# A planned attention-and-FFN kernel: the low-bits branch moves into the first batch's list, and the step lists are reordered

## The reference

```python
qkv = x @ Wqkv + bqkv
att = softmax(where(causal, q @ k.T * D ** -0.5, -inf))
x = layernorm(x + (att @ v) @ Wout + bout)
h = silu(lin(x, w1)) * lin(x, w2)          # lin: (x @ w.T) * s
h = gelu(lin(h, h1)); h = gelu(lin(h, h2))  # 1024 -> 1024
x = layernorm(x + lin(h, w3))
```

## Time and profile before

| | us |
|---|---|
| median of three runs | 2191.09 |
| fastest and slowest run | 2189.73, 2191.16 |
| the profiled execution | 2188.74 |
| its span | 2187.0 |
| PE busy in it | 2129.8 (97%) |
| ACT, DVE, POOL busy | 1317.0, 1248.7, 489.7 |

### The profile page before, as it was taken

One profiled execution on the slowest core, in us unless ns is written; L12 is line 12 of the kernel. 1 busy time (PEld: TensorE's weight loads), 2 busy tenths in 40 slices (PEclk: granted clock), 3 DMA queues, 4 the chain that ended last, 5 costly groups with the idle time before them and its releaser, 6 DMA issues.

```text
span 2187.0 us, 52042 instructions
## 1 busy us (share of the span) xinstructions
PE 2129.8 (97%) x16294; PEld 1873.9 (86%) x16294; DVE 1248.7 (57%) x3928; ACT 1317.0 (60%) x2807; POOL 489.7 (22%) x899
## 2 busy tenths in 40 slices
PE   7679999999999999999999999999999999999998
...
DMA packets 95941, 167.71 MB, mean 77 GB/s; under 512 B 19204, under 2 KB 38404, under 8 KB 95672
## 3 DMA queue, kind: packets, MB, share of 16 engines
...
...
## 4 chain that ended last, share of the span: by engine, by line
PE 88%; issue 1%; ACT 1%; SPq 1%; DVE 1%; DMA 1%; POOL 0%; ACTq 0%; DVEq 0%; POOLq 0%
PE ring L1236 44%; PE ring L1221 11%; PE pM L1111 7%; PE pS L1099 6%; PE pO L1159 6%; PE ring L1249 5%; PE ring L1171 4%; PE ring L1201 2%; PE ring L1191 2%; ACT probs_a L766 1%; PE ring L1143 1%; SPq L606 0%; DMA Qs<-nm 0%; PE ring L1210 0%; DMA rec<-rec_d 0%
## 5 line engine op out<-in xcount | busy, mean ns | idle before, releaser
L916 DVE CUSTOM_DVE_ANT_0 pM<-pM,mask 128x512 f32<-128x512 f32 (+3 forms) x1024 | 497.8, 502 | 361.6 <-PE pM L1111 298.9
L1236 PE MATMUL ring<-Yhi,H 128*128 128x256 f32 x1984 | 501.8, 290 | 0.3 <-DVE c L932 0.3
L1236 PE MATMUL ring<-Xhi,H 128*128 128x256 f32 x1984 | 497.7, 289 | 0.0
L1236 PE MATMUL ring<-Ylo,H 128*128 128x256 f32 x1984 | 487.4, 282 | 0.0
L1236 PE MATMUL ring<-Xlo,H 128*128 128x256 f32 x1984 | 486.1, 282 | 0.0
L1236 PEld LDWEIGHTS ring<-Yhi,H 128*128 128x128 f32 x1984 | 377.1, 190 | 10.6 <-issue 6.5
L1236 PEld LDWEIGHTS ring<-Ylo,H 128*128 128x128 f32 x1984 | 378.0, 190 | 6.8 <-issue 3.3
L1236 PEld LDWEIGHTS ring<-Xlo,H 128*128 128x128 f32 x1984 | 379.3, 191 | 1.4
L1236 PEld LDWEIGHTS ring<-Xhi,H 128*128 128x128 f32 x1984 | 378.4, 191 | 1.5 <-issue 0.2
L1111 PE MATMUL pM<-Ks,Qs 128*128 128x512 f32 x992 | 301.1, 343 | 16.1 <-DVE mx L916 9.4
L860 ACT ACTIVATE Yhi<-ring,cols 128x256 fp32r<-128x256 f32 x248 | 117.1, 472 | 277.3 <-PE ring L1236 155.8
...
## 6 DMA issues: line engine op xcount, KB each, us to landing
...
```

Source lines behind the costliest of these rows:

```text
L916: nc.vector.tensor_tensor_reduce(pM[:, h % 2, 0:n], pM[:, h % 2, 0:n], mask[:, T - n:T], 1.0, NEG, ALU.add, ALU.max, mx[:, t, h:h + 1]).th ...
L1236: mm = nc.tensor.matmul(to, w, x_part, start=(k == 0 and m == 0), stop=(k == KB - 1 and m == 1))
```

## The change

`weight_flag` becomes the last entry of HEAD_ORDER. The branch then stands inside pass 0: PE runs HEAD up to and with `weight_flag`, reads the flag, and each of the two variants begins with the rest of HEAD (`among=slice(flagged, None)`) and goes on with pass 1 as a whole. `ends` is replaced by a test on the slice. The ring bank of `weight_flag` is given out with the others of HEAD and no longer set by hand.

All three lists have a new order. ORDER has the same 326 steps. HEAD has three steps that were not in it, `x1_turn:0:1`, `exp:1:1:3` and `weight_flag:0`, and no longer has `o_out:1:0`, `max:1:2:3:0` and `max:1:2:3:1`, which are now in FIRST. TAIL_ORDER is as it was.

The code, and of the lists the stretches around the branch, around ffn_out and gu, and of the end of attention (the diff is cut):

```diff
 ORDER = """
...
-h_act:-2:h2:1:5 qk:0:3 h2:-2:1:6:0 ln1:-1 h_rest:-2:h2:1:6 h2:-2:1:6:1 neg_max:0:1 stack:0:3 h_act:-2:h2:1:6
-h_act:-2:h2:1:7 h_rest:-2:h2:1:7 h2:-2:1:7:0 h2:-2:1:7:1 x1_turn:-1:0 max:0:2:3:0 ffn_out:-2:1:0 ffn_out:-2:1:1
-table:0:Exp:2 exp:0:1:0 exp:0:1:1 max:0:2:3:1 x1_turn:-1:1 exp:0:1:2 exp:0:1:3 max:0:2:3:2 exp:0:1:4 max:0:2:3:3
-exp:0:1:5 gu:-1:0:0 exp:0:1:6 gu:-1:0:1 exp:0:1:7 ffn_hi:-1:0:0 gu:-1:0:2 exp:0:1:8 ffn_hi:-1:0:1 max:0:2:2:0
...
-h1:-1:0:6:1 h_rest:-1:h1:0:4 h_rest:-1:h1:0:5 h_act:-1:h1:0:6 neg_max:0:2 h_rest:-1:h1:0:6 h_act:-1:h1:0:7
-h1:-1:0:7:0 max:0:3:3:0 h_rest:-1:h1:0:7 table:0:Exp:4 max:0:3:3:1 h1:-1:0:7:1 qk:1:0 max:0:3:3:2 h2:-1:0:0:0
-exp:0:2:0 exp:0:2:1 h2:-1:0:0:1 o_out:0:1 exp:0:2:2 max:0:3:3:3 exp:0:2:3 max:0:3:2:0 h2:-1:0:1:0 exp:0:2:4
...
-h2:-1:0:7:0 h_rest:-1:h2:0:5 h2:-1:0:7:1 neg_max:0:3 h_rest:-1:h2:0:6 h_rest:-1:h2:0:7 qk:1:1 ffn_out:-1:0:0
...
-exp:0:3:9 ffn_hi:-1:1:5 gu:-1:1:7 exp:0:3:10 ffn_hi:-1:1:6 ffn_hi:-1:1:7 v:1:0 pv:0:3:1 max:1:0:2:0 max:1:0:2:1
-o_out:0:3 table:0:Gelu:7 h1:-1:1:0:0 h_act:-1:h1:1:0 v:1:1 den:0 max:1:0:2:2 max:1:0:2:3 h1:-1:1:0:1 h1:-1:1:1:0
-max:1:0:1:0 stack:1:1 h1:-1:1:1:1 max:1:0:1:1 h_rest:-1:h1:1:0 h_act:-1:h1:1:1 h1:-1:1:2:0 h_act:-1:h1:1:2
...
-h1:-1:1:6:1 neg_max:1:0 h1:-1:1:7:0 h_act:-1:h1:1:6 h_act:-1:h1:1:7 h1:-1:1:7:1 h_rest:-1:h1:1:4
-h_rest:-1:h1:1:5 neg_split:1:0 den_turn:0 h_rest:-1:h1:1:6 ln2:-1:0 qk:1:2 h_rest:-1:h1:1:7
+max:0:1:3:0 max:0:1:3:1 y:-1:0:0 table:0:Exp:0 exp:0:0:0 y:-1:0:1 max:0:1:3:2 max:0:1:3:3 exp:0:0:1 y:-1:1:0
...
+h2:-2:1:4:1 h_rest:-2:h2:1:3 neg_split:0:1 ln1:-1 qk:0:3 h_act:-2:h2:1:5 h2:-2:1:5:0 h2:-2:1:5:1 h2:-2:1:6:0
+h_rest:-2:h2:1:4 neg_max:0:1 h_rest:-2:h2:1:5 h_act:-2:h2:1:6 o_out:0:0 max:0:2:3:0 h_act:-2:h2:1:7
+h_rest:-2:h2:1:6 h2:-2:1:6:1 h2:-2:1:7:0 h2:-2:1:7:1 max:0:2:3:1 h_rest:-2:h2:1:7 x1_turn:-1:0 table:0:Exp:2
+ffn_out:-2:1:0 x1_turn:-1:1 exp:0:1:0 exp:0:1:1 ffn_out:-2:1:1 exp:0:1:2 max:0:2:3:2 exp:0:1:3 gu:-1:0:0
+exp:0:1:4 max:0:2:3:3 exp:0:1:5 gu:-1:0:1 exp:0:1:6 ffn_hi:-1:0:0 gu:-1:0:2 max:0:2:2:0 exp:0:1:7 ffn_hi:-1:0:1
...
+max:0:2:0:3 h1:-1:0:3:1 neg_split:0:2 h1:-1:0:4:0 h_rest:-1:h1:0:2 h1:-1:0:4:1 h1:-1:0:5:0 neg_max:0:2
+h1:-1:0:5:1 h_rest:-1:h1:0:3 h1:-1:0:6:0 h_rest:-1:h1:0:4 h1:-1:0:6:1 h_act:-1:h1:0:6 h_rest:-1:h1:0:5
+h_rest:-1:h1:0:6 ln2_stats:-2:1 h_act:-1:h1:0:7 h1:-1:0:7:0 table:0:Exp:4 h_rest:-1:h1:0:7 h1:-1:0:7:1
+max:0:3:3:0 qk:1:0 max:0:3:3:1 exp:0:2:0 exp:0:2:1 h2:-1:0:0:0 max:0:3:3:2 h2:-1:0:0:1 exp:0:2:2 exp:0:2:3
...
+h2:-1:0:6:1 h_rest:-1:h2:0:5 h_rest:-1:h2:0:6 h_rest:-1:h2:0:7 h2:-1:0:7:0 neg_max:0:3 h_act:-1:h2:0:7
+h2:-1:0:7:1 max:1:0:3:0 qk:1:1 ffn_out:-1:0:0 table:0:Exp:6 exp:0:3:0 max:1:0:3:1 exp:0:3:1 stack:1:1
...
+ffn_hi:-1:1:6 table:0:Gelu:7 h1:-1:1:0:0 ffn_hi:-1:1:7 pv:0:3:1 v:1:0 max:1:0:2:2 max:1:0:2:3 h_rest:-1:h1:1:0
+o_out:0:3 h1:-1:1:0:1 max:1:0:1:0 h1:-1:1:1:0 h_act:-1:h1:1:0 h_act:-1:h1:1:1 h_rest:-1:h1:1:1 den:0
...
+h1:-1:1:6:1 h1:-1:1:7:0 neg_max:1:0 den_turn:0 h_rest:-1:h1:1:7 h1:-1:1:7:1 h_act:-1:h1:1:7 qk:1:2 v:1:3
...
 HEAD_ORDER = """
...
-exp:0:3:8 weight_test:0:1 exp:0:3:9 exp:0:3:10 weight_test:0:2 weight_test:0:3 weight_test:0:4 weights:0:8
-pv:0:3:1 weight_test:0:5 weight_test:0:6 weights:0:9 o_out:0:3 max:1:0:3:0 max:1:0:3:1 qk:1:1 max:1:0:3:2
-max:1:0:3:3 max:1:0:2:0 weight_test:0:7 v:1:0 v:1:1 den:0 max:1:0:2:1 weights:0:10 max:1:0:2:2 weight_test:0:8
-max:1:0:2:3 stack:1:1 max:1:0:1:0 max:1:0:1:1 max:1:0:1:2 max:1:0:1:3 weight_test:0:9 rec_save:0 v:1:2
-rec_load:0 v:1:3 max:1:0:0:0 max:1:0:0:1 max:1:0:0:2 max:1:0:0:3 neg_split:1:0 weight_test:0:10 neg_max:1:0
...
-o_out:1:0 max:1:1:0:0 pv:1:0:1 max:1:1:0:1 max:1:1:0:2 max:1:1:0:3 neg_max:1:1 ln1_stats:0 neg_split:1:1 ln1:0
-qk:1:3 exp:1:1:0 max:1:2:3:0 max:1:2:3:1 exp:1:1:1 x1_turn:0:0 exp:1:1:2
...
+exp:0:2:8 pv:0:2:0 stack:1:0 max:0:3:0:2 exp:0:2:9 exp:0:2:10 max:0:3:0:3 weights:0:7 neg_max:0:3
+weight_test:0:2 pv:0:2:1 o_out:0:2 neg_split:0:3 exp:0:3:0 exp:0:3:1 weight_test:0:3 weight_test:0:4 exp:0:3:2
+weight_test:0:5 qk:1:1 max:1:0:3:0 weights:0:8 exp:0:3:3 exp:0:3:4 max:1:0:3:1 exp:0:3:5 max:1:0:3:2 exp:0:3:6
+exp:0:3:7 weight_test:0:6 pv:0:3:0 max:1:0:3:3 max:1:0:2:0 exp:0:3:8 weights:0:9 exp:0:3:9 exp:0:3:10
+max:1:0:2:1 pv:0:3:1 o_out:0:3 weight_test:0:7 max:1:0:2:2 max:1:0:2:3 max:1:0:1:0 v:1:0 max:1:0:1:1 max:1:0:1:2
+den:0 max:1:0:1:3 max:1:0:0:0 max:1:0:0:1 max:1:0:0:2 max:1:0:0:3 stack:1:1 neg_split:1:0 rec_save:0 neg_max:1:0
+exp:1:0:0 v:1:1 weight_test:0:8 exp:1:0:1 v:1:2 max:1:1:3:0 rec_load:0 max:1:1:3:1 max:1:1:3:2 exp:1:0:2
+max:1:1:3:3 max:1:1:2:0 exp:1:0:3 exp:1:0:4 den_turn:0 max:1:1:2:1 weight_test:0:9 max:1:1:2:2 exp:1:0:5
+raw:0:10 v:1:3 exp:1:0:6 exp:1:0:7 max:1:1:2:3 qk:1:2 exp:1:0:8 exp:1:0:9 y:0:0:0 max:1:1:1:0 max:1:1:1:1
+y:0:0:1 exp:1:0:10 max:1:1:1:2 max:1:1:1:3 y:0:1:0 y:0:1:1 max:1:1:0:0 max:1:1:0:1 ln1_stats:0 max:1:1:0:2
+weights:0:10 max:1:1:0:3 stack:1:2 neg_split:1:1 weight_test:0:10 ln1:0 low_bits:0 pv:1:0:1 neg_max:1:1 qk:1:3
+exp:1:1:0 x1_turn:0:0 exp:1:1:1 x1_turn:0:1 exp:1:1:2 exp:1:1:3 weight_flag:0
...
 FIRST_ORDER = """
-x1_turn:-1:1 exp:0:1:3 table:0:Exp:0 exp:0:1:4 table:0:Gelu:1 weight_flag:0 max:0:2:3:2 table:0:Exp:2 gu:-1:0:0
...
+table:0:Exp:0 table:0:Gelu:1 o_out:0:0 table:0:Exp:2 max:0:2:3:0 exp:0:1:4 exp:0:1:5 gu:-1:0:0 gu:-1:0:1
...
-BANKS["weight_flag", 0, ()] = BANKS["gu", -1, (0, 0)]
...
-            def iteration(i, steps, odd, taken, general, ends=True):
+            def iteration(i, steps, odd, taken, general, among=slice(None)):
...
-                for kind, off, a in steps:
+                for kind, off, a in steps[among]:
...
-                if ends:
+                if among.stop is None:
...
+            flagged = 1 + HEAD.index(("weight_flag", 0, ()))
+
             def ffn_iterations(taken, general):
-                iteration(1, first[split:], 1, taken, general)
+                iteration(0, HEAD, 0, taken, general, slice(flagged, None))
+                iteration(1, steps_of(1), 1, taken, general)
...
-            iteration(0, HEAD, 0, taken, False)
-
-            first = steps_of(1)
-            split = 1 + next(n for n, s in enumerate(first) if s[0] == "weight_flag")
-            iteration(1, first[:split], 1, taken, False, ends=False)
+            iteration(0, HEAD, 0, taken, False, slice(0, flagged))
```

113 lines of the change are left out of this document (56 added, 57 removed).

## The result

The changed kernel takes 2171.86 us (median of four runs, 2168.91 to 2173.43) against 2190.56 before (four runs, 2189.73 to 2191.16): ratio 0.9913, 95% interval 0.9896 to 0.9930. The forecast was 2175. The profiled execution took 2173.1, its span 2171.3, which is 15.7 less than the span of 2187.0 before. The medians differ by 18.7: the profiled execution before (2188.74) was faster than all four runs there, and the one after is the second slowest of its four; the spread of the runs is 1.4 us before and 4.5 after.

The account below looks back on a forecast made before the run. Head bound by waits, the rest by PE, which is held 1.0 us per pass. Profiled 2188.74 - 11.2 (loop) - 6 (head) + 1 (pass 15) = 2172.5; with 2.35 from profiled execution to median, 2175; range 2164 to 2188.

Parts of the forecast that it names:

- The loop: Between ffn_out and gu 0, 0.8 of 1.0 us held time saved in passes 2 to 15: -11.2 us, 0 to -14.
- x1Thi's copy between two exponentials: On ACT between second and third exp: said to delay the third exp and hold PE's next scores; part of 1.0 us.
- ffn_out and gu between the scores: New order puts 16 ffn_out matmuls (1.9 us) and gu 0 (0.95 us) between exps, so no scores wait.
- nm's way: Chain neg_max, nm, Qs, exp 0: becomes tighter, 0.2 us left at groups 0 and 3, no cost in the sum.
- The estimate of 4.9 us against 5.1: Unqueued need from neg_max to exp 0, 4.9 us, against PE's 5.1 us at groups 0 and 3.
- The slow rival: nm comes too late at groups 0 or 3 in 14 passes: 2197 at one, 2218 at both; chance 0.08.
- +1.0 was forecast, for den_turn: pv:0:3 after one h1 step; in pass 15 nothing fills den_turn's wait ahead of y: +1.0 us once, 0 to +1.
- The head: Stretch before the flag: less DVE work and waiting, minus later pv and o_out: -6 us, from -13 to +3.
- The rival that the head gains nothing: The tests' run holds pv:0:2:1 as before and the last weight piece takes the rest: 2181 to 2185; chance 0.16.
- The branch: weight_flag last in HEAD, the same work executed: 0 us, with -0.5 to +0.5 for another place in the code.
- o_out:1:0: Now behind the flag, so gu 0's tanh waits for Osb's copies: +0.5 us, 0 if ACT early, +2 if late.

Follow-up runs that it names:

- e3_turn: The kernel before with one ORDER step moved, x1_turn 1 from behind exp 1 of group 1 to ahead of ffn_out t=1: 2188.05 us (0.9992).
- e4_stretch: The kernel before with the stretch from ffn_out t=0 to gu 1 in the changed kernel's order, rest of ORDER old: 2204.55 us (1.0067).
- e10_stretch_qk: e4_stretch with one more step moved, qk:0:3 two h2 steps earlier, ahead of h2 5:0: 2214.23 us (1.0115).
- e12_both: The changed kernel with h_act 5 moved behind neg_max 2 and 32 already fulfilled waits on SP's queue ahead of pass 15: 2165.30 us (0.9886).
- e2_head: The changed kernel with the old ORDER, so new HEAD, FIRST and branch place alone: 2183.36 us (0.9971).
- e9_pad: The changed kernel with 32 already fulfilled waits on SP's queue, behind the loop and ahead of pass 15: 2166.39 us (0.9901).
- e8_no_branch: The changed kernel without reading the flag and the branch, PE going straight into the fast variant: 2170.39 us (0.9910).

## Why the prediction was right, and where it was not

**The loop.** 0.8 of 1.0 us a pass was taken; 0.99 came. But the reason that the prediction read from the earlier trace rows, x1Thi's copy between two exponentials, fell in e3_turn: without it the hold is the same. The part that carries is the other half of its account, ffn_out and gu between the scores: e4_stretch has the scores unheld by it. And that half is bought with the cover of nm's way (e4_stretch: +1.1 us a pass), which qk:0:3's earlier place pays for only together with what stands around it (e10_stretch_qk); in the changed kernel 0.13 us a pass of that hold is left. So the size came out right, with one of its two reasons wrong.

**nm's way.** The estimate of 4.9 us against 5.1 was close: exp 0 of group 0 starts 4.96 us after neg_max, of group 3 5.10, both with SP at 1.14, and neither is held. Pass 15 measures the need itself: there exp 0 of group 3 starts 4.69 us after neg_max, with SP at 1.05, and waits the last 0.18 of it for nm's copies; so the estimate was some 0.2 us too high. The slow rival did not come in the loop; its mechanism did come in pass 15, at group 2, which the prediction counted safe with 7.2 us. It had looked at the loop's list alone: qk:1:0 drops out in pass 15, and h_act 5 stands ahead of nm's copy on ACT.

**Pass 15.** +1.0 was forecast, for den_turn; +3.2 was measured, for another reason. The reciprocal's chain did stay in front of y (PE waits 0.68 us for it, 0.43 before). The larger part is the hold of 3.45 at exp 0, and 2.3 us come from the lower clock behind it (0.97 over the whole pass); e12_both, without both, has pass 15 at 122.5, which is 2.7 us less than before. So without them the term would have been a gain.

**The head.** -6 was forecast and -6.3 came, at the start of pass 2, in the one pair of executions; so close a match is luck, since ten executions put it at 8.4 on average, from 5.7 to 10.9. Flag at 133.26 (133 to 135 forecast; 129.90 to 133.39 in the six kernels with this HEAD), y at 116.76 (115), DVE busy for 32.19 of 40.8 us in the stretch to the flag (32.9 of 39.9). pv's last matmuls end at 93.9, 1.4 later than before (1.5). So the terms of that stretch held within 2 us each; that DVE decides there is read from these rows, not tested. The rival that the head gains nothing fell in e2_head. Its mechanism, the run of tests that holds POOL, is real but was not what held pv:0:2:1: there PE waited 3.40 us for neg_max 3, so for DVE, behind tests 1 and 2:

```profile
76.22 0.93 PE L1142 MATMUL ring<-ident,m_wide 128*98 128x128 f32 x4 [3.40 <-DVE m_wide L931]
```

**The branch.** 0, with 0.5 either way, was too narrow: the stop grew by 1.46. It was 5.48 to 7.32 us in the seven kernels with the old steps around it, and 6.17 to 8.18 in the five with the new ones (6.99 in the changed kernel, 8.18 in e9_pad, 6.17 in e12_both). One pair does not show that the change made it longer. The changed kernel's extra 1.46 us are the code's transfer, which started 1.57 later behind the flag's matmul; why it did stays open. It costs less than it lasts, since Osb's copies need most of the time, as the prediction put it for o_out:1:0 (e8_no_branch).

In the profiled execution (2173.1 against 2172.5) passes 2 to 14 gave 2.2 us more than forecast, the head 0.3 more, and pass 15 took back 3.0: that the sum came within 0.6 us is two errors that cancel, so partly luck. The median came out 3 us below the forecast because 2.35 us had been added for the way from the profiled execution to the median, and this time the median lies 1.2 below it: two of the other runs were 2.5 and 4.2 us faster than the profiled one.
